# An AdaLN block with windowed top-32 attention: gate rows and expert matrices made batch by batch in the distance banks, one masked product in place of two

## The reference, cut to what matters

```python
x = L0_attn_x                                   # (8 batches, 1024 tokens, 128)
ga = (2 * (ga >= 0) - 1) * jnp.maximum(jnp.abs(ga), 0.25)   # gate rows, one per batch; gb alike
h = _layernorm(x) * (1 + ca) + sa
dist = jnp.sqrt((diff * diff * m_h).sum(axis=-1) + 1e-08)
neg_d, loc = jax.lax.top_k(-dist, K)
infl = jnp.exp(-topd)
infl = infl / (infl.sum(axis=-1, keepdims=True) + 1e-08)
context = jnp.einsum('btk,btkd->btd', infl, neighbor_v) + gate * 0.1 * heb_ctx
outs.append(q_h * context)
x = x + ga * (concat(outs) @ decoder)
h = _layernorm(x) * (1 + cb) + sb
# feed-forward: two of 8 experts per batch, chosen by the batch's first token
gates = _gates(h[:, 0, :], Wr)
weighted = sum_e gates[b, e] * (h @ A[e].T @ Bw[e].T)
x = x + gb * (h + weighted)
```

## Time and profile before

| What | Value |
|---|---|
| median of three runs | 686.34 us |
| the profiled execution: its own time, its span | 686.94 us, 685.2 us |
| busy share of the span: PE, DVE, ACT, POOL | 90%, 88%, 76%, 71% |
| mean granted TensorE clock | 0.96 |
| scans (L1096) | 64, the first at 105.1 us, the last at 661.7 us |
| starts of L1046 and of L1052 behind it, in one step | 305.55 us, 305.74 us |
| DVE idle before the scan, with ACT L787 as releaser | 12.0 us over 35 scans |

### The profile page before, as it was taken

The page is one execution under the profiler, slowest core; times in us unless marked ns, Lnnn a source line. Parts: engine busy times, 40 slices in busy tenths (PEclk is TensorE's granted clock), DMA queues, the critical chain, the costliest instruction groups (busy, mean ns, idle before and its releaser), DMA issues. The chain is left out here.

```text
span 685.2 us, 22680 instructions
## 1 busy us (share of the span) xinstructions
PE 615.5 (90%) x6050; PEld 432.1 (63%) x6114; DVE 602.9 (88%) x4954; ACT 519.2 (76%) x1574; POOL 488.4 (71%) x717
## 2 busy tenths in 40 slices
PE   4997887899999999999999999999999999999876
PEld 2543444566776676666666666666666666667654
DVE  4895458899999999999999999999999999999860
ACT  2896125688888888888888888888888888888752
POOL 3111314788888888888888888888888888888662
PEclk9998566899999999999999999999999999999999
DMA  7220000000001010001010101010001000000000
GB/s 212 77 77 5 10 9 20 16 22 27 23 27 28 26 28 27 27 27 28 27 27 26 28 26 28 26 28 26 27 27 28 26 24 28 27 26 25 18 12 16
DMA packets 41183, 21.22 MB, mean 31 GB/s; under 512 B 6040, under 2 KB 40544, under 8 KB 41056
## 3 DMA queue, kind: packets, MB, share of 16 engines
q1 hardware_dynamic: 41056, 19.77, 10.1%
HBM read 10.44 MB, written 4.19 MB: 21 GB/s over the span
## 5 line engine op out<-in xcount | busy, mean ns | idle before, releaser
L1009 DVE MAX8 top<-modn_all 128x8 f32<-128x32 f32 x2048 | 207.1, 175 | 6.4
L562 POOL TENSOR_TENSOR big<-big,con 128x512 f32<-128x512 f32 x128 | 160.4, 1275 | 22.4 <-DVE big L1068 22.4
L1015 DVE MATCH_REPLACE8 modn_all<-top,modn_all 128x32 f32<-128x32 f32 x1024 | 166.4, 173 | 0.0
L1260 PE MATMUL psC<-vst,big 128*128 128x68 f32 x512 | 103.0, 283 | 9.7 <-POOL big L562 7.7
L502 POOL TENSOR_TENSOR wmod_sb<-key,meet 128x512 f32<-128x512 f32 x64 | 67.8, 1060 | 51.8 <-DVE meet L1096 51.8
L1261 PE MATMUL psC<-vst,big 128*128 128x68 f32 x512 | 99.7, 276 | 0.0
L1260 PEld LDWEIGHTS psC<-vst,big 128*128 128x128 f32 x512 | 78.3, 193 | 31.4 <-POOL big L562 30.6
L1261 PEld LDWEIGHTS psC<-vst,big 128*128 128x128 f32 x512 | 78.7, 194 | 0.0
L1015 DVE MATCH_VALUE_LOAD modn_all<-top,modn_all 128x8 f32 x1024 | 77.3, 75 | 0.0
L771 ACT ACTIVATE psD<-key 128x256 f32<-128x256 f32 x64 | 24.8, 388 | 51.0 <-issue 47.7
L1286 PE MATMUL psW<-sqs,selm 128*16 128x192 f32 x256 | 55.9, 343 | 2.8 <-POOL sqs L512 2.8
(11 more groups left out here) (215 smaller groups left out, 1578.4 us busy)
## 6 DMA issues: line engine op xcount, KB each, us to landing
tst<-qT_all SPq DMA_DIRECT2D x256, 17.0 KB
big<-in_x SPq DMA_DIRECT2D x16, 256.0 KB, 2.8
xs<-in_x SPq DMA_DIRECT2D x64, 64.0 KB, 1.9
out<-yo SPq DMA_DIRECT2D x64, 64.0 KB, 1.6
sst<-nst SPq DMA_DIRECT2D x128, 3.0 KB
tst<-nst SPq DMA_DIRECT2D x128, 2.0 KB
con<-in_consts SPq DMA_DIRECT2D x1, 581.5 KB, 6.8
wmod_sb<-in_wmod SPq DMA_DIRECT2D x1, 384.0 KB, 5.8
```

The source lines that it names most:

```text
L562: nc.gpsimd.tensor_tensor(wab[:, k % 2, v].rearrange("p (r t) -> p r t", r=4), wsel.rearrange("p (r t) -> p r t", r=4), part.unsqueeze(1). ...
L1009: last = v.max(top[:, u, h, where], low_high[:, u, h])
L1015: last = v.match_replace(low_high[:, u, h], top[:, u, h, 1:9], low_high[:, u, h], GONE)
L1260: mm(o, wab[:, k % 2, 0, cols], vst[:, blk + 1:blk + 3, r], start=True, stop=False)
```

## The change: what it does

1. `gate_rows` and `expert_sum` now make one batch at a time, in the unused columns of three distance banks (`pGate`), on PE directly after `distances(k)` and before `dist_ready` is signalled: two fp32 matmuls of 128 columns when k is the first chunk of a batch (8 times), five when k is the fourth (8 times; the fifth adds the identity). DVE applies them ahead of the epilogue of that chunk (`gates`, `expert`), POOL scales B by batch (`bsc`, 128x512).
2. The early routing stands elsewhere: `routing_front` and `routing_logits` in step -3, `routing_gates` at the end of PE's step -2; `gateT` is copied behind the epilogue of chunk 0, and `gate_er` in step 0. ACT L771 of chunk 0 no longer waits for the distances of chunk 1; in return PE's masks of chunk 1 wait for the pairs of chunk 0 (`pair_done`). POOL makes the squares of chunk 0 ahead of the wait for `aS_ready`.
3. The denominator's 1e-8 is added by one small PE matmul (one row of weights, 16 columns) at the end of the context, and `den` on DVE is gone.
4. The context is `w @ v_before + (w * own) @ (v_own - v_before)`: DVE writes the weights straight into `wab[.., 0]`, POOL makes the difference of values `vdif` (128x272) and one masked product in place of two.

```diff
+        pGate = [psD[:, r].rearrange("p (g x) -> p g x", g=NG)[:, :, PW + HW:PW + HW + D // 2] for r in range(3)]
...
+        pDen = pC.rearrange("p (n x) -> p n x", x=VD)[:, :, HD]
...
+        def gates_with(k):
+
+            return k // CPB if k % CPB == 0 else None
+
+        def expert_with(k):
+
+            return k // CPB if k % CPB == 3 else None
...
+            nc.gpsimd.tensor_tensor(sqs[:], first, first, ALU.mult).then_inc(opnd_ready, 1)
             pool.wait_ge(aS_ready, 1)
...
+                if there(i) and i % CPB == 0:
+                    b = i // CPB
+                    pool.wait_ge(r0_dve, 10)
+                    need(pool, gb_ready, b)
+                    nc.gpsimd.tensor_tensor(bsc[:], b_sb[:], gate_er[:, :, b:b + 1].broadcast_to([P, 4, D]),
+                                            ALU.mult).then_inc(bsc_ready, 1)
...
+                    nc.gpsimd.tensor_tensor(vdif[:, k % 2], vst[:, blk + 1:blk + 3], vst[:, blk:blk + 2],
+                                            ALU.subtract).then_inc(vdif_ready, 1)
                     pool.wait_ge(w_ready, k + 1)
-                    need(pool, c_ready, k - 1)
-                    for v, part in enumerate((of_own, of_before)):
-                        nc.gpsimd.tensor_tensor(wab[:, k % 2, v].rearrange("p (r t) -> p r t", r=4),
-                                                wsel.rearrange("p (r t) -> p r t", r=4),
-                                                part.unsqueeze(1).broadcast_to([P, 4, CH]), ALU.mult).then_inc(wab_ready, 1)
...
+                    nc.gpsimd.tensor_tensor(wab[:, k % 2, 1].rearrange("p (r t) -> p r t", r=4),
+                                            wab[:, k % 2, 0].rearrange("p (r t) -> p r t", r=4),
+                                            of_own.unsqueeze(1).broadcast_to([P, 4, CH]), ALU.mult).then_inc(wab_ready, 1)
...
-                    act.wait_ge(dist_ready, min(k + 2, NCH))
+                    if k:
+                        act.wait_ge(dist_ready, min(k + 2, NCH))
...
-                    v.tensor_scalar(den[:, s], cst[:, s, :, HD], 1e-8, None, ALU.add).then_inc(den_done, 1)
...
+                    if gates_with(k) is not None:
+                        gates(gates_with(k))
+                    if expert_with(k) is not None:
+                        expert(expert_with(k))
                     e = key[:, k % 2].rearrange("p (h j) -> p h j", h=NH)
                     v.scalar_tensor_tensor(out=e, in0=pB, scalar=0.0, in1=e, op0=ALU.max, op1=ALU.min).then_inc(d2_ready, 1)
...
+                    pe.wait_ge(w_ready, k + 1)
+                    context(0, vst[:, blk:blk + 2], True)
+                    pe.wait_ge(vdif_ready, k + 1)
+                    pe.wait_ge(wab_ready, k + 1)
+                    last = context(1, vdif[:, k % 2], False)
+                    last = mm(pDen, con[0:1, C_ID:C_ID + 1].broadcast_to([1, P]),
+                              con[0:1, C_TINY:C_TINY + 1].broadcast_to([1, 4 * NG * 2]), start=False, stop=True,
+                              skip_group_check=True)
                     last.then_inc(c_ready, 1)
...
+                    if k == 1:
+                        pe.wait_ge(pair_done, 2)
                     for r in range(NR):
                         masks(r)
-                    distances(k % 2).then_inc(dist_ready, 1)
+                    last = distances(k % 2)
+                    if gates_with(k) is not None:
+                        last = gate_rows(gates_with(k))
+                    if expert_with(k) is not None:
+                        last = expert_sum(expert_with(k))
+                    last.then_inc(dist_ready, 1)
```

More of the change, by code:

```diff
@@ L1214, in _, with routing_gates @@
+            def routing_gates():
+                pe.wait_ge(r0_dve, 8)
+                nc.tensor.transpose(psX[0:NE, 152:152 + NB], s8[:, 20], con[0:NB, 0:NB]).then_inc(r0_pe, 1)
+                pe.wait_ge(r0_dve, 9)
+                for kt in range(4):
+                    last = mm(psX[:, 160 + kt * NB:160 + (kt + 1) * NB], con[0:NE, C_EXP + kt * P:C_EXP + (kt + 1) * P],
+                              gateT[:], start=True, stop=True)
+                last.then_inc(r0_pe, 1)
             encv_a = encv_sb[:].rearrange("p (r a e) -> p a r e", r=4, a=2)
@@ L1233, in distances, with gate_rows, expert_sum @@
                 return last
+            def gate_rows(b):
+                for u in range(2):
+                    last = mm(pGate[u], con[0:NB, b:b + 1].broadcast_to([NB, P]), gn[:, u].rearrange("b (g x) -> b g x", g=NG),
+                              start=False, stop=True, skip_group_check=True)
+                return last
+            def expert_sum(b):
+                pe.wait_ge(bsc_ready, b + 1)
+                for kt in range(4):
+                    mm(pGate[2], a_sb[:, kt], bsc[:, kt].rearrange("p (g x) -> p g x", g=NG), start=False, stop=False,
+                       skip_group_check=True)
+                return mm(pGate[2], ident, ident.rearrange("p (g x) -> p g x", g=NG), start=False, stop=True,
+                          skip_group_check=True)
             def keep_clock(bank, width, times):
@@ L1255, in step, with context @@
                     keep_clock(psC, PW, {NCH: 0, NCH + 1: 9}.get(i, 3))
-                    pe.wait_ge(wab_ready, 2 * k + 2)
-                    for r in range(4):
-                        cols = slice(r * P, (r + 1) * P)
-                        o = pC[:, r * 2 * VP:(r + 1) * 2 * VP].rearrange("p (v x) -> p v x", v=2)
-                        mm(o, wab[:, k % 2, 0, cols], vst[:, blk + 1:blk + 3, r], start=True, stop=False)
-                        last = mm(o, wab[:, k % 2, 1, cols], vst[:, blk:blk + 2, r], start=False, stop=True)
+                    def context(part, values, first):
+                        for r in range(4):
+                            o = pC[:, r * 2 * VP:(r + 1) * 2 * VP].rearrange("p (v x) -> p v x", v=2)
+                            done = mm(o, wab[:, k % 2, part, r * P:(r + 1) * P], values[:, :, r], start=first and r == 0,
+                                      stop=not first, skip_group_check=True)
+                        return done
+                    pe.wait_ge(w_ready, k + 1)
[5 more added lines that the diff above has]
+                              con[0:1, C_TINY:C_TINY + 1].broadcast_to([1, 4 * NG * 2]), start=False, stop=True,
+                              skip_group_check=True)
                     last.then_inc(c_ready, 1)
@@ L1281, in step @@
                 k = i + 3
+                if k == 0:
+                    routing_front()
+                    pe.wait_ge(selm_ready, 2)
                 if there(k):
@@ L1348, in step @@
                     nc.tensor.transpose(pO, osp[:, k % 2], ident).then_inc(po_ready, 1)
-            steps(step, routing)
+            steps(step)
 def kernel(**inputs):
```

153 lines of the change are left out of this document (53 added, 100 removed).

## The result

The changed kernel takes 697.22 us (median of four runs, 694.64 to 700.55), against 686.24 us for the kernel before on the same chip: ratio 1.017, 95% interval 1.012 to 1.021. It is slower. The forecast was 691.0 us with a range of 685 to 695, so the sign was right and the size too small.

What follows compares the result with a forecast made beforehand. A ring of scan, POOL, ACT, PE, ACT was taken to bound the loop, with DVE outside but for the scan. +10.8 - 1.6 + 2.2 - 7.0 = +4.4, rounded up to +4.7, on 686.3 gave 691.0 us, range 685 to 695.

Steps and rivals of the forecast that it cites:

- The ring: Loop step: closed chain scan, POOL, ACT, PE, ACT, scan without slack, 8.64 us, charging added PE work in full.
- D: Rival, loop: batch matmuls hide because ACT idles 0.71 us before L771 and catches up; 680 us, chance 0.10.
- C: Rival, loop: DVE was the bound, so 0.19 us per chunk leaves each of 58 steps; 679 us, chance 0.06.
- 8.73 us steps: Every fourth loop step: context waits 0.24 us for POOL's second product; one masked product frees 16 x 0.1 us.
- The batch matmuls: Loop, PE between distances and `dist_ready`: gate rows 0.44 us, expert sum 1.10 us, seven batches, +10.8 us.
- The small matmul: End of PE's context: takes 0.2 us, lengthens the ring by some 0.05 us in 43 steps, +2.2 us.
- The masked product and `den`: Loop, POOL and DVE: one masked product gives -1.6 us; dropping `den` is worth 0.
- The front: Start of the kernel through the first scan and the next steps: -7.0 us in all, first scan at 97.1.
- the exchange: Front: masks of chunk 1 wait for the pairs of chunk 0, +1.9 us on PE.
- B: Rival, front: the clock comes back before the second scan, about 3 us less; 688 us, chance 0.18.
- E: Rival, front: it gives only -3 us because chunks 0 and 1 run one after the other; 695 us, chance 0.16.
- A: Main case, whole kernel: the ring pays for every batch, the front gives 7; 691 us, 689 to 693, chance 0.50.

Runs made afterwards that it cites:

- e10: e6 plus one 8-row, 128-column matmul per step that nothing reads, directly behind the distances; 700.9 us, ratio 1.021.
- e1: The changed kernel with `den` back on DVE and PE's one-row matmul for 1e-8 removed; 691.0 us, ratio 1.008.
- e2: The changed kernel with the small matmul for 1e-8 taking 128 rows of weights in place of one; 688.4 us, ratio 1.003.
- e4: The kernel before with only the fourth part of the change, one masked product in place of two; 686.8 us, ratio 0.999.
- e11: e6 plus one 128-row, 128-column matmul per step that nothing reads, directly behind the distances; 692.4 us, ratio 1.007.
- e7: e2 with the gate rows also made with 128 rows, their operand padded with zeros; 688.2 us, ratio 1.001.
- e3: The kernel before with DVE's `den` left out and nothing in its place, so 1e-8 is missing; 684.6 us, ratio 0.999.
- e8: e6 without the exchange of waits between chunks 0 and 1 in the front; 673.1 us, ratio 0.979.
- e6: The changed kernel with `den` on DVE, no small matmul, and batch matmuls ahead of the context in place of filler; 674.5 us, ratio 0.985.
- e6b: e6 unchanged, run again as the base on the same chip as e8; 673.9 us, ratio 0.980.

## Why the prediction was right in sign and short in size

**The ring: right.** Ordinary, gate and expert steps grew by what PE's pieces on the ring take, and DVE gained idle time, 0.26 us per scan on average. e10 refutes D: ACT caught up none of 57 delays. e1 refutes C as the account of the whole loop, since DVE with more work left ordinary steps at 8.63. That "the only DVE piece in it is the scan" was too strong all the same: behind the gate rows e1's DVE came last, for 0.2 us in one step of eight, and in the 8.73 us steps of before it stood on the way to POOL's products.

**The batch matmuls: mechanism right, term mis-sized.** I had 7 x 1.54 = 10.8 us. Measured, against the step of their kin in e2: 9.55 - 8.91 = 0.64 for the gate rows and 9.79 - 8.63 = 1.16 for the expert sum, 1.80 a batch, 12.6 us. It is the difference of the loops of e2 and e4 too (509.1 - 496.5). POOL's `bsc`, which I had put at nothing, cost nothing: the 1.16 us of the expert step are what five matmuls take (0.27 for the first by e11, 0.22 for each further one). The matmuls of the earlier trace rows, by which I priced them, have full weights. Of the 0.20 us that the gate rows cost above my 0.44, 0.15 is the price of their 8 rows, by e7.

**The small matmul: the step that failed.** I wrote "it has 128-column weights like the latter, so I take 0.2", and +0.05 us a step, +2.2, with bounds of 0 to +3. It costs 0.42 us at its place and 5.7 us in the loop: 0.12 in an ordinary step and 0.24 in the expert step. The bounds came from rows of 18 and of 128 rows of weights, and one row lies outside both. The "0.15 us that ACT is late" was too small a slack as well (it is 0.3), but the price was wrong by more. The Trainium skill (TensorE: Matmul & The Clock Gate, section LDWEIGHTS) has it that a weight load goes by columns, not rows; my 0.2 agreed with the estimate by that page, and I took this as a second witness. The same page of the Trainium skill (section Why this matters for your kernels) says that a single matmul with 32 rows takes the time of one with 128. No run here has 32 rows; of 1 and of 8 rows it doesn't hold at these places, by the kernel after against e2 and by e10 against e11: 0.42 against 0.20 us, and 0.41 against 0.27.

**The masked product and `den`: -1.6 and 0, right as a sum.** But `den` alone at 0 was wrong: e3 gains the 1.6 us by it, so they could as well have been booked there.

**The front: -6.9 us where I had -7.0, by luck.** Four kernels have this front, and their fourth scans came at 129.21 (after), 128.35 (e1), 124.74 (e2) and 128.71 (e7), 6.9 to 11.4 us ahead of the 136.09 before; and the old front moved as well, to 134.99 in e3 and 139.08 in e4. In the one profile of after, two errors of mine cancel. The first scan came at 98.75, not 97.1 (where my sum also had 91.1 for a term of 91.0). Gate rows of batch 0 ended at 78.7 us and not at 76.6, because the second norms of chunk 0 stand behind two routing matmuls that wait 1.83 and 0.46 us for DVE. The gates (L1185) followed at 80.88 instead of 78.95, and the masks of chunk 1 at 86.28, after a wait of 1.61 for the exchange, which I had put at +1.9 (e8 gives 1.6). The timeline of PE in the kernel after:

```profile
72.36 0.27 PE L1175 MATMUL psX<-con,z_all 8*128 8x8 f32 x1 [1.83 <-DVE z_all L950]
73.09 0.21 PE L1177 MATMUL psX<-wr_sb,h0T 128*8 128x8 f32 x2 [0.46 <-DVE h0T L953]
73.15 1.44 PE L1288 MATMUL psW<-sqs,selm 128*16 128x192 f32 x4
...
77.52 1.22 PE L1213 MATMUL psD<-gn,con 8*128 8x128 f32 x4
...
80.88 1.87 PE L1185 MATMUL psX<-gateT,con 8*128 8x8 f32 x8 [2.13 <-DVE gateT L1044]
...
86.28 1.23 PE L1196 MATMUL psD<-mask_bf,ident_bf 128*128 128x320 bf16 x4 [1.61 <-DVE modn_all L1020]
```

The loss of 1.65 came back, to 0.1, after the first scan. I had put those three steps at +1.05 us against before, and they took 0.5 us less (30.46 against 30.96). Before, the clock fell a second time behind the first scan and stayed at 1.2 GHz until 123.4; after, it was at 2.4 GHz from 111.2 on. I had allowed 0.6 us for that.

**B, the clock: wrong as an alternative, right as a thing that happens.** In the profile of after it didn't come: the distances behind the first scan still take 1.37 us (at 106.22, the granted clock rises at 111.2). In the profile of e2, whose front is the same, they take 0.80 (timeline of PE):

```profile
103.86 0.80 PE L1206 MATMUL psD<-sst,tst 18*64 18x160 f32 x32
```

The clock rose at 102.6 there, and the second scan follows the first by 10.5 us instead of 13.7. That is the "about 3 us" of B. It isn't a property of the kernel: e6 and e6b are one kernel, and their clock rose at 110.9 and at 104.2, their spans 673.9 and 670.9 us. What sets the moment stays open. Between these two profiles it is worth 3 us, no less than what a front edit is worth. How much of the spread of the medians it makes is not shown: in e2's ten runs the mean granted clock and the time don't go together (686.12 us at 0.964, 689.07 at 0.968).

**The range.** Its top was E's 695, a case of the front. The chance that A's own terms are all short in one direction had no room in it, and this is what came: 1.8 us of batch matmuls and 3.5 of the small one, 5.3 of the 5.4 us by which the loop exceeds the forecast.

## What to carry to other kernels

When an edit puts work on an engine inside the ring, look for the kind of instruction in a row of the same shape, rows of weights too; where none is there, the bounds must reach above the nearest row, not end at it. Before moving work onto a critical arc, ask whether the same engine has filler elsewhere in the step: the same matmuls cost 12.6 us behind the distances and 0.2 in the place of filler. If a matmul of a few rows stands on the path, pad it with zeros to 128 rows and look at the step: here that took 0.15 us off the step with two of them (e7). And an engine outside the ring has only its slack: DVE idles 0.38 us ahead of an ordinary scan, and not at all behind the gate rows. Before a front's gain is read from a single profile, the spread of that front over profiles has to be known, here 4.5 us.

## What the runs showed of the hardware that was not expected

An fp32 matmul with 1 or 8 rows of weights held up what follows it longer than one with 128 rows at the same place: 0.42 against 0.20 us at 16 columns (1 row, between matmuls of 128 rows), 0.41 against 0.27 at 128 columns (8 rows, behind the distances of 18 rows and ahead of transposes of 128). A second one of 8 rows behind the first adds 0.22, the price of the earlier trace rows. What makes it so stays open.

The moment at which the granted clock comes back to 2.4 GHz after the front varies from 102.6 us (e2) to 111.3 us (e11) over kernels whose fronts are nearly alike, and from 104.2 to 110.9 between two executions of the same one.
